# Cycles of sixteen gathered groups and one picked group in a graph layer on one core

## The reference

```python
h = jnp.maximum(_layernorm(x, axis=-1), 0.0)
# in the layer, with x = h
x_i = x[dst]
x_j = x[src]
tmp = jnp.concatenate([x_i, x_j, edge_attr], axis=1)
h = jax.nn.relu(tmp @ W1 + b1)
msg = h @ W2 + b2
out = jax.ops.segment_sum(msg, dst, num_segments=N_NODES)
# and at the end
x = x + out
```

## Time and profile before

| | |
|---|---|
| timed runs (3) | median 3469.36 us, 3468.13 to 3474.51 |
| span of the profiled execution | 4774.3 us |
| PE busy | 3927.4 us, 82% |
| PEld busy | 3397.9 us, 71% |
| DVE busy | 2554.6 us, 54% |
| ACT busy | 2043.4 us, 43% |
| POOL busy | 2613.2 us, 55% |
| mean granted clock of PE | 0.850 |

### The profile page before, as it was taken

The page is one execution under the profiler, slowest core; times in us unless marked ns, Lnnn a source line. Parts: engine busy times, 40 slices in busy tenths (PEclk is TensorE's granted clock), DMA queues, the critical chain, the costliest instruction groups (busy, mean ns, idle before and its releaser), DMA issues.

```text
span 4774.3 us, 95161 instructions
## 1 busy us (share of the span) xinstructions
PE 3927.4 (82%) x21992; PEld 3397.9 (71%) x21992; DVE 2554.6 (54%) x5906; ACT 2043.4 (43%) x7414; POOL 2613.2 (55%) x2766
## 2 busy tenths in 40 slices
PE   3788888888888888888888888888888888888887
PEld 3677777777777777777777777777777777777776
DVE  3655555565555555555555555555555555555553
ACT  2444444444444444444444444444444444444443
POOL 5455555555555555555555555555555555555555
PEclk9988888888888888888888888888888888888886
DMA  4522222222222222222222222222222222222223
GB/s 146 142 80 72 75 78 79 78 78 75 76 77 76 78 74 75 76 78 76 76 75 74 77 77 77 76 76 73 77 74 77 75 77 73 78 75 79 74 79 81
DMA packets 286658, 380.47 MB, mean 80 GB/s; under 512 B 90916, under 2 KB 190549, under 8 KB 285542
## 3 DMA queue, kind: packets, MB, share of 16 engines
q0 software_dynamic: 88064, 177.91, 14.7%
q1 hardware_dynamic: 198342, 201.58, 14.6%
q10 hardware_dynamic: 208, 0.49, 0.1%
HBM read 362.58 MB, written 17.04 MB: 80 GB/s over the span
## 4 chain that ended last, share of the span: by engine, by line
another core or an unknown queue 30%; issue 19%; DVE 18%; PE 14%; DVEq 11%; SPq 4%; ACT 4%; DMA 1%; ACTq 0%
PE ps L1310 6%; DVEq L1004 5%; DVE lhs L992 5%; PE ps L1286 3%; PE ps L1294 3%; DVE gath L1001 2%; DVE work L1047 2%; DVE onehot L979 2%; DVE p_hot L1025 2%; ACT work L674 2%; DVE nodes L1014 2%; SPq L411 1%; SPq L412 1%; DVEq L1093 1%
## 5 line engine op out<-in xcount | busy, mean ns | idle before, releaser
L535 POOL DMA_INDIRECT gath<-b_table,idx x2688 | 2549.3, 948 | 2127.3 <-ACT idx L639 1294.6
L1310 PE MATMUL ps<-h_tab,p_hot 128*128 128x480 f32 (+1 forms) x6768 | 1944.0, 431 | 259.5 <-issue 255.7
L1310 PEld LDWEIGHTS ps<-h_tab,p_hot 128*128 128x128 f32 x6768 | 1449.9, 226 | 467.6 <-issue 344.3
L674 ACT ACTIVATE work<-ps,work 128x80 f32<-128x80 f32 x4136 | 1039.1, 408 | 1675.3 <-remote 1458.2
L1286 PE MATMUL ps<-rhs,lhs 96*128 96x128 f32 x5376 | 906.6, 316 | 270.1 <-DVE gath L1001 124.3
L1286 PEld LDWEIGHTS ps<-rhs,lhs 96*128 96x128 f32 x5376 | 785.3, 219 | 403.1 <-issue 331.8
L1014 DVE TENSOR_TENSOR nodes<-ps,nodes 48x48 f32 x768 | 153.7, 200 | 1611.5 <-remote 1490.1
L1294 PE MATMUL ps<-onehot,gath 128*128 128x48 f32 x5376 | 799.6, 295 | 88.4 <-ACT gath L655 75.0
L1294 PEld LDWEIGHTS ps<-onehot,gath 128*128 128x128 f32 x5376 | 783.1, 221 | 109.1 <-ACT gath L655 95.0
L1025 DVE TENSOR_TENSOR p_hot<-work,ps 128x1152 fp32r<-128x1152 f32 x376 | 506.6, 1347 | 57.7 <-PE ps L1310 34.0
L992 DVE TENSOR_SCALAR_CACHE_REDUCE lhs<-nodes 48x512 f32<-48x512 f32 (+1 forms) x768 | 520.0, 677 | 32.0 <-issue 5.7
(11 more groups left out here) (128 smaller groups left out, 1640.8 us busy)
## 6 DMA issues: line engine op xcount, KB each, us to landing
nodes<-dst_row SPq DMA_DIRECT2D x494, 96.0 KB
gath<-b_table,idx POOLq DMA_INDIRECT x2688
nodes<-dst_row SPq DMA_DIRECT2D x384, 72.0 KB
lhs<-in_edge_t SPq DMA_DIRECT2D x384, 64.0 KB
work<-key_row SPq DMA_DIRECT2D x94, 256.0 KB
lhs<-in_edge_t SPq DMA_DIRECT2D x384, 48.0 KB
rhs<-a_table SPq DMA_DIRECT2D x768, 24.0 KB
work<-in_edge_t SPq DMA_DIRECT2D x220, 32.0 KB
```

Source lines behind the costliest of these rows:

```text
L535: pool.indirect_dma_start(gath[:, u, t, :], None, b_table, bass.IndirectOffsetOnAxis(ap=idx[:, u, t:t + 1], axis=0)).then_inc(gathered[u], 16)
L674: m = nc.scalar.activation(p_sel[:, t % 2, :, at_j], ps_run[:, q, j * words:(j + 1) * words], ACT.Copy, scale=p_mask[:, at_j, t:t + 1])
L1310: mm = nc.tensor.matmul(ps_run[:, q, 0:m * words].rearrange("p (j w) -> p j w", j=m), p_hot[:, t % 2, i, :], h_tab[:, first:first + BLOCKS ...
```

## The change

A cycle has sixteen steps in place of eight and still one picked group. Its eight runs move to the odd steps, one whole run in each, and the calls that make, pick and use it are set to other steps. There are 50 cycles for 95 and 16 steps after them for four, so that the edges still fit (five tiles of padding for three): 2870 gathered tiles, 49 picked groups and 16 early ones. The picked group's output is now added within the cycle that follows its runs, not in the one after. The counting of covered edges takes one cycle of 16 steps for two of eight. The front part of the output is stored from step 23 of the last cycle.

```diff
-PERIOD = 8
+PERIOD = 16
...
-CYCLES = 95
-EXTRA = 4
+CYCLES = 50
+EXTRA = 16
...
-PAD_TILES = 3
-COUNT_PIECES = 16
+PAD_TILES = 5
+COUNT_PIECES = PERIOD
...
-                    sp.wait_ge(p_out_added, place_p(items - 1, 0))
+                    sp.wait_ge(p_out_added, place_p(items - 1, 0) + 1)
...
-                    if final and j >= 3 + EXTRA:
-                        store_front(j - 3 - EXTRA)
+                    if final and 0 <= j - 7 - EXTRA < pieces:
+                        store_front(j - 7 - EXTRA)
...
-                    if j == (4 if c <= EARLY else 0) and not first:
+                    if j == (6 if c <= EARLY else 0) and not first:
                         load_tail(p_group(c - 1, it), p_tile(c - 1, it), place_p(c - 1, it))
-                    if j == PERIOD - 1 and more:
+                    if j == PERIOD - 2 and more:
                         load_key(c + 1, it)
...
-                    if j == 0 and not first:
+                    if j == 1 and not first:
                         pick(runs - 1, c - 1, it)
-                    if j > 0 and not final:
-                        pick(j - 1, c, it)
+                    if j % 2 and 1 < j < PERIOD and not final:
+                        pick((j - 3) // 2, c, it)
...
-                    if j == 0 and c > 1:
-                        copy_sums_tail(place_p(c - 2, it))
+                    if j == 10 and not first:
+                        copy_sums_tail(place_p(c - 1, it))
...
-                    if j == 0 and not first:
-                        sum_picked(2, c - 1, it)
-                    if j == 1 and not final:
-                        key_hot(1, c, it)
-                    if j == 2 and not first:
+                    if j == 4 and not first:
                         sum_picked(3, c - 1, it)
                         unpack_words(c - 1, it)
-                    if j == 3 and not first:
+                    if j == 5 and not first:
                         dst_hot_t_tail(p_group(c - 1, it), place_p(c - 1, it))
-                    if j == 3 and not final:
-                        key_hot(2, c, it)
-                    if j == 4 and not final:
-                        sum_picked(0, c, it)
+                    if j in (3, 7, 11) and not final:
+                        key_hot((j + 1) // 4, c, it)
+                    if j in (6, 10, 14) and not final:
+                        sum_picked((j - 6) // 4, c, it)
...
-                    if j == 3 and not first:
+                    if j == 5 and not first:
                         turn_p(c - 1, it)
...
-                    if j == 5 and not first:
+                    if j == 7 and not first:
                         make_z_tail(place_p(c - 1, it))
-                    if j == 7 and not first:
+                    if j == 9 and not first:
                         make_sums_tail(place_p(c - 1, it))
...
-                    if not final:
-                        run_p(j, c, it)
+                    if j % 2 and not final:
+                        run_p(j // 2, c, it)
...
-                    if j == 0 and c > 1:
-                        fold_tail(place_p(c - 2, it))
+                    if j == 10 and not first:
+                        fold_tail(place_p(c - 1, it))
```

More of the change, by code:

```diff
@@ L85, in gnn @@
     assert n_tiles == ALL_TILES and cycles > EARLY + 5
-    assert BLOCKS * PARTS >= node_tiles and RUN_PARTS[0] * words <= BANK and runs == PERIOD
-    assert PERIOD == 2 * SLOTS and LEAD == SLOTS and early_tiles == EARLY_A + EARLY_B + EARLY_C
+    assert BLOCKS * PARTS >= node_tiles and RUN_PARTS[0] * words <= BANK and 2 * runs == PERIOD
+    assert PERIOD == 4 * SLOTS and LEAD == SLOTS and early_tiles == EARLY_A + EARLY_B + EARLY_C
     assert rounds * gen_cols * gen_k == n_nodes and front_piece * pieces == front
@@ L127, in gnn @@
         p_deg = sb("p_deg", [P, 1])
-        key_sb = sb("key_sb", [P, 3, p_cols])
+        key_sb = sb("key_sb", [P, 3, max(p_cols, chunk_tiles * whole // 2)])
         key_iota = sb("key_iota", [P, BLOCKS])
@@ L355, in _ @@
             sp.dma_start(src_sb[:, early_tiles:n_tiles], src_t[:, early_tiles:n_tiles]).then_inc(src_in, 16)
-            sp.dma_start(key_sb[:, 0, :].bitcast(I32), src_p).then_inc(src_in, 16)
+            sp.dma_start(key_sb[:, 0, 0:p_cols].bitcast(I32), src_p).then_inc(src_in, 16)
             for s in range(SLOTS):
@@ L398, in _ @@
                     sp.wait_ge(key_step, 4)
-                    sp.dma_start(key_row, key_sb[:, 2, :]).then_inc(key_stored, 16)
+                    sp.dma_start(key_row, key_sb[:, 2, 0:p_cols]).then_inc(key_stored, 16)
                     sp.wait_ge(dst_row_stored, 16)
@@ L720, in cycle @@
                         rectify_tail(place_e(c - 1, it), c == 1)
-                    if j == 4 and not first:
+                    if j == 6 and not first:
                         keep_tail_h(place_p(c - 1, it))
@@ L726, in cycle @@
                                              ).then_inc(early_std, 1)
-                    if c == 1 and j == 5:
+                    if c == 1 and j == 13:
                         act.wait_ge(early_ready, 4)
-                    if j == 5 and c < EARLY:
+                    if j == 13 and c < EARLY:
                         keep_early(c, it)
-                    if j == 6 and not first:
+                    if j == 8 and not first:
                         rectify_tail(place_p(c - 1, it))
@@ L757, in _ @@
                     copy_sums(k - 3, 0)
-                if k == fetched:
-                    copy_sums_tail(place_p(items - 1, 0))
             act.wait_ge(flag_ready, 1)
@@ L892, in split_keys @@
                 dve.wait_ge(src_in, 32)
-                src_f, part_f, key_f = key_sb[:, 0, :].bitcast(I32), key_sb[:, 1, :], key_sb[:, 2, :]
+                src_f, part_f, key_f = (key_sb[:, n, 0:p_cols] for n in range(3))
+                src_f = src_f.bitcast(I32)
                 nc.vector.tensor_scalar(part_f, src_f, 1.0 / span, 0.25 / span - 0.5, ALU.mult, ALU.add).then_inc(key_step, 1)
@@ L1103, in cycle @@
                         add_z(k - 3, it)
-                    if j == 0 and not first:
-                        sum_picked(2, c - 1, it)
-                    if j == 1 and not final:
-                        key_hot(1, c, it)
-                    if j == 2 and not first:
+                    if j == 4 and not first:
                         sum_picked(3, c - 1, it)
                         unpack_words(c - 1, it)
-                    if j == 3 and not first:
+                    if j == 5 and not first:
                         dst_hot_t_tail(p_group(c - 1, it), place_p(c - 1, it))
-                    if j == 3 and not final:
-                        key_hot(2, c, it)
-                    if j == 4 and not final:
-                        sum_picked(0, c, it)
+                    if j in (3, 7, 11) and not final:
+                        key_hot((j + 1) // 4, c, it)
+                    if j in (6, 10, 14) and not final:
+                        sum_picked((j - 6) // 4, c, it)
                     if j == 0 and 0 < c <= EARLY:
                         dst_hot_tail((c - 1 + it) * TILES, place_e(c - 1, it), c == 1)
-                    if j == 4 and not first:
+                    if j == 6 and not first:
                         dst_hot_tail(p_tile(c - 1, it), place_p(c - 1, it))
[L1121 to L1125, removed]
+                    if j == PERIOD - 1 and more:
                         key_hot(0, c + 1, it)
@@ L1131, in cycle @@
                         beside, after = None, None
-                        if c > 1:
-                            beside, after = {1: (place_p(c - 2, it), None), 3: (None, place_p(c - 2, it))}.get(j, (None, None))
+                        if not first:
+                            beside, after = {11: (place_p(c - 1, it), None), 13: (None, place_p(c - 1, it))}.get(j, (None, None))
                         if ends_e and j == 5:
@@ L1140, in cycle @@
                         add_out(k - 4, it, after, beside)
-                    if j == 1 and c > 1:
-                        add_out_tail(p_group(c - 2, it), place_p(c - 2, it), it, k - 4)
+                    if j == 11 and not first:
+                        add_out_tail(p_group(c - 1, it), place_p(c - 1, it), it, k - 4)
                     if j == 5 and ends_e:
                         add_out_tail(c - 1 + it, place_e(c - 1, it), it, k - 4)
-                    if j == 7 and c < EARLY:
+                    if j == PERIOD - 1 and c < EARLY:
                         dst_hot_t_tail(c + it, place_e(c, it), first)
-                    if j == 0 and not final:
+                    if j == 2 and not final:
                         part_masks(c, it)
@@ L1152, in cycle @@
                         write_last_early()
-                    if c in (EARLY, EARLY + 1):
-                        count_inside((c - EARLY) * PERIOD + j)
+                    if c == EARLY:
+                        count_inside(j)
```

(7 more changed lines are left out.)

## The result

| | median us | runs |
|---|---|---|
| before | 3468.74 | 3467.39 to 3474.51 (4) |
| after | 3695.07 | 3694.39 to 3695.47 (3 of 4) |
| ratio | 1.0653 | 95% interval 1.0638 to 1.0668 |

The forecast was 3697 us. The fourth run of the changed kernel took 4361.53 us with a mean granted clock of 0.551 in place of 0.82; it has no trace, so it stays open whether PE bound it at the lower clock (the prediction's wholly cold case, 4520 us) or stalls like those of e1 did, and it is left out of the ratio. The profiled execution of the changed kernel took 3694.68 us with a span of 3692.8 us, so unlike that of the kernel before it is one of the timed kind.

A forecast was written before the change was run, and what follows sets the result against it. The prediction took POOL's indirect gathers as the bound of the timed run and summed 87.4 + 2870 x 1.2509 + 12.9 + 6.7 = 3697 us, +6.6% against 3469, with a range of 3650 to 3785 us.

The forecast's parts named there:

- the prediction's wholly cold case: Rival's extreme: PE at its lower clock throughout becomes the bound, 4520 us; PE's clock costing time had 0.12 in all.
- The bound: POOL's gathers, one each 1.2509 us, fill the timed run before the change; PE has 8% of slack.
- The attribution of the stalls: PE's stalls belong to the profiled execution, not the timed ones; the new profile's span would be 4250 to 4750 us.
- POOL's path: Kernel before: first table gather at 87.4 us, 2688 gathers at 1.2509 us, 12.9 us after the last: 3462.7 us.
- the 6.7 us that were left over: Rest between POOL's summed 3462.7 us and the timed median of 3469.4 us, carried into the forecast sum.
- The mix: Gathered tiles go from 2688 to 2870; 182 more gathers on POOL's path at 1.2509 us cost 227.7 us.
- PE alone: Kernel before, if PE bound it: 95 cycles of 32.3 us plus some 100, 3170 us, 300 us less than timed.
- PE's savings, ACT's and DVE's: Net 717 us off PE, plus fewer picking copies, wide one-hots and reductions on ACT and DVE; all worth 0.
- Runs in odd steps, moved steps, slots: Denser odd steps, moved loads and stores, and gather slots coming back in time: each taken as 0; moved steps 0 to +10 us.
- The clock: Rival: emptier PE falls to its lower clock and delays POOL, likelier as lags, +140 us to 3837 us; chance 0.12.
- Every step would be cold: The Trainium skill's rule applied to PE: waiting between batches, it would start each step at the low clock.
- POOL faster without the profiler: Rival: part of the 0.30 us between gathers is the profiler's; below 1.171 us each the kernel gets faster; chance 0.04.

The follow-up runs named there:

- e1: Kernel before, unchanged, profiled again, on the chip with the stalls: 4783.86 us; seven timed runs there had a median of 4784.39 us.
- f1: Kernel before, unchanged, profiled again on another chip, without the stalls: 3475.49 us, beside a median of 3468.00 us in 13 timed runs.
- g3: Kernel before with three gathers in place of four in every step of four tiles (results wrong): 3228.95 us, ratio 0.9309.
- f2: Kernel before with one matmul in place of nine in each picking run (picked rows wrong), without the stalls: 3480.66 us, ratio 1.0040.
- g4: Changed kernel with one matmul in place of nine in each picking run (picked rows wrong): 3694.29 us, ratio 1.0651.
- f3: Changed kernel with the nine matmuls of each picking run done twice, result kept, without the stalls: 3707.39 us, ratio 1.0680.
- g1: Changed kernel, unchanged, measured again: 3696.19 us, ratio 1.0657.
- g2: Kernel before with one more gather in every fourth step, 192 in all, into a buffer nobody reads: 3706.44 us, ratio 1.0685.
- f4: Changed kernel with three gathers in place of four in every step of four tiles (results wrong): 3239.98 us, ratio 0.9342.

## Why the prediction was right, point by point

*The bound.* Right, and for the reason given: POOL's rhythm is the same in every execution (944 to 947 ns, one gather each 1.250 to 1.253 us when nothing holds it), and of the profile with stalls only stretches without a wait were used for it. The busy shares of the earlier trace rows would have named PE, and the waits of the earlier trace rows with them as the prediction read them (the rows say "remote" and do not name PE), and 717 us less work on PE would then have read as a gain.

*The attribution of the stalls.* Wrong. The prediction tied them to being profiled and expected them in the next profile; e1 and f1 show that they came with the chip or its condition. The forecast did not hang on it, because the sum used only intervals without a stall. What did hang on it failed: the span of the new profile was to be 4250 to 4750 us and was 3692.8 us.

*POOL's path.* The profiled execution measures it as 93.3 to the first gather, 2869 x 1.2504 to the last, 12.2 from there to the span's end (3692.8 - 3680.6) and 1.9 from the span to the time of 3694.68 us. The front was 5.9 us under what it is, since POOL, not PE, sets when the table's gathers start and some of the front's gathers took 1.0 to 2.5 us in place of 0.94; the 6.7 us that were left over were for the most part this. That the front's other transfers made them longer would be a guess.

*The mix.* 182 gathers for 227.7 us; measured 226.3.

*PE alone.* Its 3170 us for the kernel before were some 60 us too few, by g3's 3229: the "some 100" in the sum is too little for the front, the steps after the last cycle and the early groups. The slack was 240 us and not 300; nothing in the forecast changes by it.

*PE's savings, ACT's and DVE's.* Worth nothing, as said: f2 and g4 take a further 1295 and some 675 us off PE without gain, f3 adds about as much as the change had saved and loses 0.3%, most of it in gathers 3 ns longer, as f1 has them too.

*Runs in odd steps, moved steps, slots.* 0 was right within what can be measured: the change's price per gather, 1.244 us (1.250 in g1), is 6 to 12 ns above that of g2, which leaves 1 to 2 us for all of them, less than the interval of the ratio (5 us to either side).

*The clock.* The mean fell to 0.82, as said, and did not cost. (It fell from the 0.990 of f1; the 0.850 of the profile before held the stalls.) The prediction's limit, 72% of the time at the lower clock, wasn't reached (0.82 is 36% of it). But an average was the wrong measure: f4 loses 54 us at a mean of 0.89, with PE at 46.6 of 60.0 us, all of it in the 16 cycles with an early group, and nothing in later cycles at the same mean. The rule of the Trainium skill (TensorE: Matmul & The Clock Gate, HAM oscillation) that a batch after a wait starts cold is borne out by the changed kernel's timeline above, at 2020.06 us behind a wait of 2.59 us; the steps at 2015.17 and 2027.45 us, with no wait for data ahead of them, ran at full clock. "Every step would be cold" was too much: the page says it of waits that are long enough, a condition that the prediction left out. In the changed kernel the cold steps have no price. The share of PE "well under 82%" was wrong (84%): the 82% held the stalls (without them the kernel before has 93%), and matmuls at half clock fill part of the gaps.

*POOL faster without the profiler.* Excluded by g2: the spacing in timed runs is 1.24 us.

## What to carry to other kernels

Where two engines share work by a ratio, write both bounds per cycle in the same unit and move the ratio toward the engine with slack: here POOL had 35.0 and PE 32.3 us per 32 tiles, and the change went to 70.0 against 46.6 per 60. Busy shares hide which engine binds when the gap between its instructions isn't counted (POOL reads 75% when it is full). The chain of the page doesn't name it either; that of the changed kernel is

```profile
PE 32%; POOL 29%; issue 23%; DMA 10%; DVE 3%; ACT 2%; DVEq 1%; SPq 0%; POOLq 0%; ACTq 0%
```

The number to trust is the spacing of an engine's instructions over a stretch without waits, times their count. If it closes to the timed median within a few us the engine is very likely the bound, and a run like g2, which adds work to that engine alone, shows it. By the same sums seven gathered groups to one picked would stand at about 30.6 against 30.5 us for 28.5 tiles, some 2% less per tile than before; that is an estimate and was not run.

## What was not expected of the hardware

- One chip ran the unchanged kernel at 4784 us, where others ran it at 3468 us, with gathers of the same length (944 and 947 ns) and waits of some 5 us each between the instructions of DVE and ACT.
- A PE with less work can cost time: one matmul in place of nine in the runs of the kernel before brought the mean clock from 0.990 to 0.641 and the kernel from 3468.0 to 3480.7 us.
- An indirect gather on POOL takes 944 to 947 ns in the median of every profile, beside a busy and an emptier PE, in a kernel 4784 us long and in one 3468 us long; in steady stretches the gap to the next is 0.30 to 0.31 us. The 3 ns between the two medians are 8 us of a whole execution.
- The same mean clock of 0.90 cost 38 gathers' time in one stretch of f4 and none in the next. POOL's waits came behind steps at half clock that carried the early group's work as well.
